# A gated cross-attention and expert kernel: layer 0's score operands in two row tiles, maxima and score halves placed side by side, gelu one sub-step later

## The chip, the core and the metric

The kernel runs on one core of a Trainium2 chip. The metric is device time in microseconds of that core; lower is better. TensorE (PE) multiplies and writes PSUM; VectorE (DVE), ScalarE (ACT) and GpSimd (POOL) do the rest; the sync engine (SP) holds a queue that issues every DMA transfer in program order.

## What is computed

Two layers, each of a cross-attention and an expert FFN, on x of 16 batches x 56 rows x 128 and a context of 16 x 1500 x 128. Sixteen heads of 8.

```python
x = x + tanh(g_xattn[0]) * xattn0(layernorm(x), ctx)            # no mask
x = x + tanh(g_ffn[0])   * ffn0(layernorm(x))                   # 8 experts of 512, top 2, exact gelu
x = x + tanh(g_xattn[1]) * xattn1(layernorm(x), ctx, mask)      # mask over the 1500 keys
x = x + tanh(g_ffn[1])   * ffn1(layernorm(x))                   # 8 experts of 64, and a shared one
# xattn: softmax(q k^T / sqrt(8)) v, heads joined, @ Wo + bo
```

## The kernel before

Batches go through in 32 steps: step n is batch n % 16 of layer n // 16, and steps run two at a time in a pipeline. In step s PE takes the maxima of batch s, the scores of batch s-1 (with a tail of batch s-2), weighs V with the exponentials, projects K for batch s+1 and V for batch s, and on odd and even steps does the small work of the FFN of the two batches that came before (`fy_uses`, `fh_uses`: experts `y0` to `y3`, hidden parts `h0` to `h7`, transposes, the query `q`).

A step has twelve sub-steps kt. Each has two maxima, two score halves and, in even kt, one weighing; K projections stand at kt 2, 4, 6 and V projections at kt 8, 9, 10.

- **Maximum** (`max_scores`, L1010): for one of 8 head pairs and one of 3 chunks of 500 keys, a matmul `qmax`^T `kop` into one of the two buffers of `pMX`. VectorE reduces it to a column of `mx` (L920, L925). 24 in a step. The maxima become shifts (`cc`, transposed to `ct`) that are written as two more rows of `qexp`.
- **Score half** (`score_half`, L972): the scores of 125 keys for four of the eight pairs, keys on the output's partitions, into one half of `pST`; ScalarE takes the exponential into `P` (L678). Half h of the next tile waits until half h is read.
- **Weighing** (`weigh`, L993): four matmuls of 17 columns at a time, on four column tiles, into `pO`.
- **Projection** (L1115 K, L1124 V) into the single `pKV`, which ScalarE copies out (L691, L696).

Queries and keys are split in a high and a low half float, so an operand has three blocks of 16 rows (a pair is 2 heads of 8): `kop` = khi, klo, khi and `qmax` = qhi, qhi, qlo. Behind them stand 56 mask rows and 2 shift rows, in layer 0 too, where the mask rows are zero: a maximum has 104 rows, a score 106. `kop`, `qmax` and `qexp` have two buffers, taken by n % 2.

SP's order in a step: the shifts to `qexp` (L474), the third part of the keys (L462), `qmax` copied to `qexp` (L486), the next context (L493), the first part of the next batch's keys, `qmax` of the next batch (L508, six transfers), the second part of the keys. The first part of the keys waits for the last score half of kt 6, which frees its buffer; the first maximum of the next step waits for `qmax` (`qmax_in`) and these keys (`kop_in[0]`).

In even steps from 4 on, kt 10 has the experts' second matmuls: `y0`, a maximum, `y1` (L1082), which wait for gelu. ScalarE does gelu at the end of kt 8, between two loads of its function table (L715, L678).

## Time and profile before

| | |
|---|---|
| median of 3 runs | 1040.72 us (1039.66 to 1044.62) |
| the profiled execution, its own time | 1040.23 us |
| its span, first to last instruction | 1038.1 us |
| TensorE busy / load of weights | 89% / 65% |
| VectorE, ScalarE, GpSimd busy | 70%, 56%, 51% |
| mean share of the 16 DMA engines | 49% |
| granted TensorE clock, mean | 0.981 |

The spans in this table and all views below are of one profiled execution. A row's duration for a matmul reaches to its modelled end, while the next one already runs; what a matmul costs PE is the distance from its start to the next start. "[1.17 <-ACT HR L715]" is idle time of the engine ahead of the row, and what ended it. SPq is the issue of a transfer on the SP queue, not the transfer. The granted clock is 1.00 from 200 us to the last matmuls.

### The profile page before, as it was taken

How to read it: one execution, taken by the hardware profiler on the slowest of the kernel's cores; microseconds unless marked ns; L12 is line 12 of the kernel's file. 1: busy time of each engine (PE TensorE's matmuls, PEld its weight loads, DVE VectorE, ACT ScalarE, POOL GpSimd, SP SyncE). 2: the span in 40 equal slices, each digit the busy share in tenths (PEclk: the TensorE clock that was granted, in tenths of full speed). 3: DMA queues.
4: the chain of work that ended last, by engine and by line, in shares of the span. 5: the costliest groups of instructions: out<-in, count | busy, mean ns of one | idle time of the engine just before them, and what ended most of it. 6: DMA issues, size and time to landing. Idle time of an engine off the chain costs nothing.

```text
span 1038.1 us, 32346 instructions
## 1 busy us (share of the span) xinstructions
PE 922.5 (89%) x13088; PEld 675.9 (65%) x13088; DVE 723.0 (70%) x1531; ACT 586.2 (56%) x1060; POOL 525.0 (51%) x667
## 2 busy tenths in 40 slices
PE   2487899999999999999999999999999999999974
PEld 0154577777777777777777777666666666666753
DVE  3376576785767768586785867878787878787722
ACT  1044556556565565656547565665757575757560
POOL 5353445543546335453446565665657576672202
PEclk9998899999999999999999999999999999999995
DMA  8735653333323333233465646767676767665200
GB/s 181 133 90 137 145 126 72 72 83 69 63 55 85 70 77 76 37 81 70 95 137 88 143 110 132 162 123 156 124 152 122 145 130 146 137 137 97 52 2 18
DMA packets 95215, 107.24 MB, mean 103 GB/s; under 512 B 22394, under 2 KB 86972, under 8 KB 95068
## 3 DMA queue, kind: packets, MB, share of 16 engines
q1 hardware_dynamic: 95068, 105.19, 49.0%
q8 instruction: 103, 1.69, 0.8%
q14 instruction: 44, 0.36, 0.1%
HBM read 35.89 MB, written 0.46 MB: 35 GB/s over the span
## 4 chain that ended last, share of the span: by engine, by line
PE 66%; DVE 16%; ACT 9%; issue 5%; SPq 2%; DMA 1%; POOL 0%; POOLq 0%; ACTq 0%; DVEq 0%
PE pO L993 13%; PE pMX L1010 12%; PE pST L972 12%; PE pKV L1124 6%; PE pFY L1082 6%; PE pKV L1115 5%; PE pFH L1150 5%; DVE mx L925 4%; DVE mx L920 4%; ACT P L678 3%; DVE rden L839 3%; PE pFY L1047 2%; ACT HR L715 1%; PE pFY L1086 1%; ACT V L696 1%
## 5 line engine op out<-in xcount | busy, mean ns | idle before, releaser
L678 ACT ACTIVATE P<-pST 125x448 f32<-125x448 f32 x768 | 396.1, 542 | 349.9 <-PE pST L972 344.3
L925 DVE TENSOR_REDUCE mx<-pMX 112x1 f32<-112x500 f32 x384 | 258.4, 673 | 172.3 <-PE pMX L1010 172.1
L1010 PE MATMUL pMX<-kop,qmax 104*112 104x500 f16 x768 | 293.1, 392 | 44.7 <-DMA qmax<-qlo 18.5
L972 PE MATMUL pST<-qexp,kop 106*128 106x112 f16 (+1 forms) x3072 | 280.2, 214 | 19.9 <-ACT P L678 9.3
L972 PEld LDWEIGHTS pST<-qexp,kop 106*128 106x128 f16 (+1 forms) x3072 | 209.9, 102 | 127.1 <-issue 42.9
L920 DVE TENSOR_REDUCE mx<-pMX 112x1 f32<-112x500 f32 x384 | 255.8, 666 | 42.8 <-PE pMX L1010 41.9
L993 PE MATMUL pO<-P,V 125*17 125x112 f32 x6144 | 186.0, 262 | 0.0
L993 PEld LDWEIGHTS pO<-P,V 125*17 125x17 f32 x6144 | 136.8, 98 | 46.2 <-issue 36.3
L1010 PEld LDWEIGHTS pMX<-kop,qmax 104*112 104x112 f16 x768 | 99.0, 132 | 93.1 <-issue 21.7
L563 POOL CAST khi<-kfull 128x500 f16<-128x500 f32 x96 | 57.7, 601 | 193.0 <-ACT kfull L691 192.8
L565 POOL TENSOR_TENSOR klo<-kfull,khi 128x500 f16<-128x500 f32 x96 | 109.0, 1135 | 7.8
L654 POOL TENSOR_TENSOR Clo<-C,Chi 128x500 f16<-128x500 f32 x93 | 105.8, 1138 | 7.5
L691 ACT ACTIVATE kfull<-pKV,W 128x500 f32<-128x500 f32 x96 | 65.0, 677 | 49.2 <-PE pKV L1115 41.1
L652 POOL CAST Chi<-C 128x500 f16<-128x500 f32 x93 | 56.6, 608 | 54.9 <-PE pKV L1124 43.8
L610 POOL TENSOR_TENSOR OM<-OM,rden 128x224 f32<-128x224 f32 x32 | 21.1, 658 | 119.6 <-DVE rden L839 119.6
L1150 PE MATMUL pFH<-xnfT,w1a 128*128 128x112 f32 x512 | 71.6, 283 | 0.0
L1124 PE MATMUL pKV<-Whi,Chi 128*128 128x128 f16 (+1 forms) x384 | 70.9, 222 | 0.7
L1082 PE MATMUL pFY<-w2a,HR 128*112 128x128 f32 x512 | 62.4, 275 | 9.4 <-ACT HR L715 9.4
L1124 PE MATMUL pKV<-Whi,Clo 128*128 128x128 f16 (+1 forms) x384 | 70.4, 221 | 0.0
L1124 PE MATMUL pKV<-Wlo,Chi 128*128 128x128 f16 (+1 forms) x384 | 70.3, 221 | 0.0
L1082 PEld LDWEIGHTS pFY<-w2a,HR 128*112 128x112 f32 x512 | 58.3, 177 | 11.5 <-issue 11.2
L696 ACT ACTIVATE V<-pKV 125x512 f32<-125x512 f32 x96 | 57.3, 597 | 14.5 <-PE pKV L1124 5.6
(144 smaller groups left out, 1089.6 us busy)
## 6 DMA issues: line engine op xcount, KB each, us to landing
C<-in_ctxT SPq DMA_DIRECT2D x32, 750.0 KB, 6.2
kop<-khi SPq DMA_DIRECT2D x192, 125.0 KB
kop<-maskop SPq DMA_DIRECT2D x48, 437.5 KB
kop<-klo SPq DMA_DIRECT2D x96, 125.0 KB
qexp<-qmax SPq DMA_DIRECT2D x32, 182.0 KB
maskin<-in_mask SPq DMA_DIRECT2D x8, 656.2 KB, 6.2
kop<-maskop SPq DMA_DIRECT2D x2, 1312.5 KB
qmax<-qhi SPq DMA_DIRECT2D x128, 7.0 KB
```

Of the source, the lines that this page charges most:

```text
L565: nc.gpsimd.tensor_tensor(klo[:, cols], kfull[:, c, :], khi[:, cols], ALU.subtract).then_inc(klo_done, 1)
L654: nc.gpsimd.tensor_tensor(Clo[:, s % 2, cols], C[:, cols], Chi[:, s % 2, cols], ALU.subtract).then_inc(ctx_split, 1)
L678: nc.scalar.activation(P[0:KP, slot, h * 4 * T:(h + 1) * 4 * T], pST[0:KP, h, 0:4 * T], ACT.Exp, scale=EXP_SCALE).then_inc(exp_done, 1)
L696: nc.scalar.activation(V[0:KP, s % 2, 4 * c:4 * c + 4, :, 0:PR].rearrange("k t p i -> k (t p) i"), pKV[0:KP, :].rearrange("k (m i) -> k m ...
L920: nc.vector.tensor_reduce(mx[:, s % 2, m // PAIRS, m % PAIRS:m % PAIRS + 1], pMX[0:T, 0, 0:CW], AX.X, ALU.max).then_inc(max_done, 1)
L925: nc.vector.tensor_reduce(mx[:, s % 2, m // PAIRS, m % PAIRS:m % PAIRS + 1], pMX[0:T, 1, 0:CW], AX.X, ALU.max).then_inc(max_done, 1)
L972: mm = nc.tensor.matmul(pST[0:cols, h, i * T:(i + 1) * T], kop[0:ROWS, b, p, tile * KP:tile * KP + cols], qexp[0:ROWS, b, p, :, :].rearran ...
L993: mm = nc.tensor.matmul(pO[32 * g:32 * g + VW, r * T:(r + 1) * T], V[0:KP, b, tile, p, :], P[0:KP, tile % RING, p * T:(p + 1) * T], start= ...
L1010: nc.tensor.matmul(pMX[0:T, m % 2, 0:CW], qmax[0:SHIFT0, st.s % 2, p, :, :].rearrange("r j q -> r (j q)"), kop[0:SHIFT0, st.s % 2, p, c * ...
L1082: mm = nc.tensor.matmul(o, HR[:, F0C * e + c, :], w2a[:, e, c, :], start=(c == 0), stop=(c == F0C - 1))
L1124: mm = nc.tensor.matmul(pKV[0:rows, i * D:(i + 1) * D], x_[:, s % 2, cols], m[:, l, 1, :], start=(k == 0), stop=(k == 2))
L1150: mm = nc.tensor.matmul(pFH[:, c * T:(c + 1) * T], w1a[:, e, c * 128:(c + 1) * 128], xnfT[:, :], start=True, stop=True)
```

## The change

In layer 0 the operands lose the mask rows and have 48 rows (50 with the shifts). Pairs 0 to 3 stand in rows 0 to 49, pairs 4 to 7 in rows 64 to 113, so `kop`, `qmax` and `qexp` use half their free size there, and a matmul touches one half of the rows. The weights' columns are put in that order at the start. Every transfer that fills these operands in layer 0 is now two, one for each half; layer 1's two shift rows and its query mask rows are written when batches 16 and 17 come. The fills of mask and pick at the start go.

On PE, a layer 0 sub-step is: a maximum of rows 64 on, the score half of rows 0 on, weighing, projection, a maximum of rows 0 on, the score half of rows 64 on, small work. Where the experts `y0`, `y1` stand (kt 10 of even steps, both layers), the projection comes before them and both score halves after them. ScalarE does gelu at the end of kt 9 instead of kt 8, and at kt 10 of even steps copies V before the exponential. `XF0` goes (its value is put in `xnf`).

```diff
+SHIFT0_L0 = 3 * PR
+ROWS_L0 = SHIFT0_L0 + 2
+HALF = 64
+HP = PAIRS // 2
+SHW = CW // 2
...
+def opens_layer(n):
+
+    return n in (B, B + 1)
+
+
+def b_total(n, c):
+
+    return sum(96 if layer_of(t) == 0 else 80 if opens_layer(t) and c == CH - 1 else 64 for t in range(n + 1))
+
+
+def q_total(n):
+
+    return sum(192 if layer_of(t) == 0 else 112 if opens_layer(t) else 96 for t in range(n + 1))
+
+
+def qexp_total(n):
+
+    return sum(32 if layer_of(t) == 0 else 16 for t in range(n % 2, n + 1, 2))
...
-            sp.wait_ge(init_v, 1)
-            sp.wait_ge(init_p, 5)
+            sp.wait_ge(init_p, 2)
             for b in range(2):
-                sp.dma_start(kop[MASK0:SHIFT0, b, :, :],
-                             maskop[0:S, :].unsqueeze(1).broadcast_to([S, PAIRS, S2])).then_inc(init_dma, 16)
-                for i in range(2):
-                    sp.dma_start(kop[SHIFT0 + i:SHIFT0 + i + 1, b, :, :],
-                                 shift_rows[:, i:i + 1, :].broadcast_to([1, PAIRS, S2])).then_inc(init_dma, 16)
-                sp.dma_start(qmax[MASK0:SHIFT0, b, :, :, :],
-                             pick[:, :, :].rearrange("s (p j) q -> s p j q", j=2)).then_inc(init_dma, 16)
+                for h in range(2):
+                    row = HALF * h + SHIFT0_L0
+                    sp.dma_start(kop[row:row + 2, b, 0:HP, :].rearrange("r p (i n) -> r (p i) n", n=SHW),
+                                 shift_rows[:, :].unsqueeze(1).broadcast_to([2, HP * S2 // SHW, SHW])
+                                 ).then_inc(init_dma, 16)
...
-                    sp.dma_start(kop[row:row + PR, dst, :, cols], part[:, cols]).then_inc(kop_in[c], 16)
+                    if n < B:
+                        for h in range(2):
+                            at = HALF * h + row
+                            sp.dma_start(kop[at:at + PR, dst, 0:HP, cols], part[HALF * h:HALF * (h + 1), cols]
+                                         ).then_inc(kop_in[c], 16)
+                    else:
+                        sp.dma_start(kop[row:row + PR, dst, :, cols], part[:, cols]).then_inc(kop_in[c], 16)
                 if n >= B:
                     half = S * (n % 2)
                     sp.dma_start(kop[MASK0:SHIFT0, dst, :, cols],
                                  maskop[half:half + S, cols].unsqueeze(1).broadcast_to([S, PAIRS, CW])
                                  ).then_inc(kop_in[c], 16)
+                if opens_layer(n) and c == CH - 1:
...
-                    sp.dma_start(qexp[SHIFT0:ROWS, (s - 1) % 2, :, :, :].rearrange("r p j q -> r (p j q)"),
-                                 ct[:, :]).then_inc(shift_in, 16)
+                    for h in range(2):
+                        if layer_of(s - 1) == 0:
+                            row = HALF * h + SHIFT0_L0
+                            to = qexp[row:row + 2, (s - 1) % 2, 0:HP, :, :]
+                        else:
+                            to = qexp[SHIFT0:ROWS, (s - 1) % 2, HP * h:HP * (h + 1), :, :]
+                        sp.dma_start(to.rearrange("r p j q -> r (p j q)"), ct[PAIRS * h:PAIRS * (h + 1), :]
+                                     ).then_inc(shift_in, 16)
...
-                    sp.dma_start(qexp[0:SHIFT0, s % 2, :, :, :], qmax[0:SHIFT0, s % 2, :, :, :]).then_inc(qexp_in[s % 2], 16)
+                    if layer_of(s) == 0:
+                        for h in range(2):
+                            rows = slice(HALF * h, HALF * h + SHIFT0_L0)
+                            sp.dma_start(qexp[rows, s % 2, 0:HP, :, :], qmax[rows, s % 2, 0:HP, :, :]
+                                         ).then_inc(qexp_in[s % 2], 16)
+                    else:
+                        sp.dma_start(qexp[0:SHIFT0, s % 2, :, :, :], qmax[0:SHIFT0, s % 2, :, :, :]
+                                     ).then_inc(qexp_in[s % 2], 16)
...
-                            sp.dma_start(qmax[row + HD * j:row + HD * (j + 1), (s + 1) % 2, :, j, :],
-                                         part[64 * j:64 * (j + 1), half:half + S]).then_inc(qmax_in, 16)
+                            if s + 1 < B:
+                                for h in range(2):
+                                    at, of = HALF * h + row + HD * j, HALF * h + HALF // 2 * j
+                                    sp.dma_start(qmax[at:at + HD, (s + 1) % 2, 0:HP, j, :],
+                                                 part[of:of + HALF // 2, half:half + S]).then_inc(qmax_in, 16)
+                            else:
+                                sp.dma_start(qmax[row + HD * j:row + HD * (j + 1), (s + 1) % 2, :, j, :],
+                                             part[64 * j:64 * (j + 1), half:half + S]).then_inc(qmax_in, 16)
+                    if opens_layer(s + 1):
+                        sp.dma_start(qmax[MASK0:SHIFT0, (s + 1) % 2, :, :, :].rearrange("s p j q -> s (p j) q"),
+                                     pick[:, :].unsqueeze(1).broadcast_to([S, H, S])).then_inc(qmax_in, 16)
...
+                for kt in range(KT):
+                    side_by_side = False
+                    if has_f(s) and kt == 10:
+                        evacuate(kt)
+                    exps(st, kt, 0)
+                    if not side_by_side and not (has_f(s) and kt == 10):
+                        evacuate(kt)
                     exps(st, kt, 1)
+                    if side_by_side and not (has_f(s) and kt == 10):
+                        evacuate(kt)
...
-                    if kt == 8 and has_f(s):
+                    if kt == 9 and has_f(s):
...
+                def largest(m):
+
+                    c, i = divmod(m, PAIRS)
+                    p = HP * (1 - m % 2) + i // 2 if layer_of(s) == 0 else i
+                    nc.vector.tensor_reduce(mx[:, s % 2, c, p:p + 1], pMX[0:T, m % 2, 0:CW], AX.X, ALU.max
+                                            ).then_inc(max_done, 1)
...
+                for i in range(HP):
+                    if layer_of(n) == 0:
+                        rows, slot = slice(HALF * h, HALF * h + ROWS_L0), i
+                    else:
+                        rows, slot = slice(0, ROWS), HP * h + i
+                    mm = nc.tensor.matmul(pST[0:keys.stop - keys.start, h, i * T:(i + 1) * T],
+                                          kop[rows, b, slot, keys],
+                                          qexp[rows, b, slot, :, :].rearrange("r j q -> r (j q)"),
...
+                if layer_of(n) == 0:
+                    h = 1 - m % 2
+                    rows, slot = slice(HALF * h, HALF * h + SHIFT0_L0), i // 2
+                else:
+                    rows, slot = slice(0, SHIFT0), i
+                nc.tensor.matmul(pMX[0:T, m % 2, 0:CW], qmax[rows, b, slot, :, :].rearrange("r j q -> r (j q)"),
+                                 kop[rows, b, slot, c * CW:(c + 1) * CW], start=True, stop=True).then_inc(mx_ready, 1)
...
+                    m0 = MAXES_PER_KT * kt
+                    together = has_m(s) and layer_of(s) == 0
+                    apart_ = has_m(s) and layer_of(s) == 1
                     late = kt in (1, 7)
-                    if has_m(s) and not late:
-                        max_scores(st, MAXES_PER_KT * kt)
-                    weigh(st, kt)
                     experts = [u[1] for u in fy_uses(s) if u[0] == kt and early(u[1])]
                     if experts:
+                        if has_m(s):
+                            max_scores(st, m0)
+                        weigh(st, kt)
+                        project(kt)
                         small("y0")
                         if has_m(s):
-                            max_scores(st, MAXES_PER_KT * kt + 1)
+                            max_scores(st, m0 + 1)
                         small("y1")
-                    score_half(st, kt, 0)
-                    if has_m(s) and late:
-                        max_scores(st, MAXES_PER_KT * kt)
-                    for use in [u[1] for u in kv_uses(s) if u[0] == kt]:
-                        c = int(use[1])
-                        free(kv_free, kv_uses, use)
-                        if use[0] == "k":
-                            if s == -1:
-                                pe.wait_ge(init_c, 2 * LAYERS + c + 1)
-                            else:
-                                pe.wait_ge(ctx_split, st.at(lambda s: CH * s + c + 1))
-                            b, l, cols = (s + 1) % 2, layer_of(s + 1), slice(c * CW, (c + 1) * CW)
-                            for i, (m, x_) in enumerate(((Whi, Chi), (Whi, Clo), (Wlo, Chi))):
-                                mm = nc.tensor.matmul(pKV[:, 0:CW], m[:, l, 0, :], x_[:, b, cols],
-                                                      start=(i == 0), stop=(i == 2))
-                        else:
-                            l = layer_of(s)
-                            for i in range(KPC):
-                                first = (KPC * c + i) * KP
-                                rows = min(KW, S2 - first)
-                                cols = slice(first, first + rows)
-                                for k, (x_, m) in enumerate(((Chi, Whi), (Chi, Wlo), (Clo, Whi))):
-                                    mm = nc.tensor.matmul(pKV[0:rows, i * D:(i + 1) * D], x_[:, s % 2, cols], m[:, l, 1, :],
-                                                          start=(k == 0), stop=(k == 2))
-                        mm.then_inc(kv_ready, 1)
-                    if has_m(s) and not experts:
-                        max_scores(st, MAXES_PER_KT * kt + 1)
-                    score_half(st, kt, 1)
+                        score_half(st, kt, 0)
+                        score_half(st, kt, 1)
+                    elif together:
+                        max_scores(st, m0)
+                        score_half(st, kt, 0)
+                        weigh(st, kt)
+                        project(kt)
+                        max_scores(st, m0 + 1)
+                        score_half(st, kt, 1)
```

The first place is kt 6 of an even step of layer 0 on PE (pMX is a maximum, pST a score half, pO a weighing, pKV a projection). Before:

```order
L1010 MATMUL pMX<-kop,qmax 112x500
L993 MATMUL pO<-P,V 17x112 x16
L972 MATMUL pST<-qexp,kop 128x112 x4
L1115 MATMUL pKV<-Chi,Whi 128x500
L1115 MATMUL pKV<-Clo,Whi 128x500
L1115 MATMUL pKV<-Chi,Wlo 128x500
L1010 MATMUL pMX<-kop,qmax 112x500
```

And after the change:

```order
L1109 MATMUL pMX<-kop,qmax 112x500
L1067 MATMUL pST<-qexp,kop 128x112 x4
L1088 MATMUL pO<-P,V 17x112 x16
L1141 MATMUL pKV<-Chi,Whi 128x500
L1141 MATMUL pKV<-Clo,Whi 128x500
L1141 MATMUL pKV<-Chi,Wlo 128x500
L1109 MATMUL pMX<-kop,qmax 112x500
L1067 MATMUL pST<-qexp,kop 128x112 x4
```

The score half has moved ahead of the weighing, next to the first maximum. The second place is kt 10 of an even step on PE; pFY are `y0` and `y1`. Before:

```order
L1010 MATMUL pMX<-kop,qmax 112x500
L993 MATMUL pO<-P,V 17x112 x16
L1082 MATMUL pFY<-w2a,HR 112x128 x8
L1010 MATMUL pMX<-kop,qmax 112x500
L1082 MATMUL pFY<-w2a,HR 112x128 x8
L972 MATMUL pST<-qexp,kop 128x112 x4
```

And after the change, from the last matmuls of the projection on:

```order
L1150 MATMUL pKV<-Wlo,Chi 125x128
L1150 MATMUL pKV<-Whi,Clo 125x128
L1204 MATMUL pFY<-w2a,HR 112x128 x8
L1109 MATMUL pMX<-kop,qmax 112x500
L1204 MATMUL pFY<-w2a,HR 112x128 x8
L1067 MATMUL pST<-qexp,kop 128x112 x8
```

The projection stood between the two score halves and stands now ahead of `y0`; the halves come together at the end. The third place is the SP queue of one step of layer 0, from the next context to the second part of the keys. Before:

```order
L493 DMA C<-in_ctxT 128x1500
L462 DMA kop<-khi 16x8x500
L462 DMA kop<-klo 16x8x500
L462 DMA kop<-khi 16x8x500
L508 DMA qmax<-qhi 8x8x56 x4
L508 DMA qmax<-qlo 8x8x56 x2
L462 DMA kop<-khi 16x8x500
```

And after the change:

```order
L540 DMA C<-in_ctxT 128x1500
L489 DMA kop<-khi 16x4x500 x2
L489 DMA kop<-klo 16x4x500 x2
L489 DMA kop<-khi 16x4x500 x2
L560 DMA qmax<-qhi 8x4x56 x8
L560 DMA qmax<-qlo 8x4x56 x4
L489 DMA kop<-khi 16x4x500 x2
```

Each transfer has become two of half the pairs.

## Rows read from the trace of the kernel before

**Rows 1.** The page, busy time of each engine (us, share, instructions).
```profile
PE 922.5 (89%) x13088; PEld 675.9 (65%) x13088; DVE 723.0 (70%) x1531; ACT 586.2 (56%) x1060; POOL 525.0 (51%) x667
```
**Rows 2.** Windows: an odd and an even step of layer 0, first maximum to first maximum.
```profile
305.20:335.50 30.30, 29.48 (x432) 22.78 (x430) 22.24 (x48) 16.62 (x33) 16.04 (x24) 1.00 0.38 83
335.50:368.50 33.00, 30.84 (x443) 24.33 (x441) 23.57 (x49) 20.59 (x33) 13.21 (x17) 1.00 0.29 58
```
**Rows 3.** The chain that ended last, from 76.1 us (start, us, what).
```profile
76.13 0.20 PE pST L972 x4
76.33 0.21 PE pMX L1010
...
76.74 0.71 PE pKV L1124 x12
```
**Rows 4.** Timeline, TensorE, a sub-step with weighing (start, us, engine, line, what).
```profile
352.04 0.38 PE L1010 MATMUL pMX<-kop,qmax 104*112 104x500 f16 x1
352.34 0.96 PE L993 MATMUL pO<-P,V 125*17 125x112 f32 x32
353.24 0.37 PE L972 MATMUL pST<-qexp,kop 106*128 106x112 f16 x4
```
**Rows 5.** Timeline, TensorE, two matmuls of 9 rows and what follows.
```profile
318.61 0.47 PE L1066 MATMUL pFY<-b2x,gateT 9*112 9x128 f32 x2
319.00 0.32 PE L1138 MATMUL pFH<-ident,xnq 112*128 112x112 f32 x1
```
**Rows 6.** Timeline, VectorE, two maxima with work waiting.
```profile
354.50 0.67 DVE L925 TENSOR_REDUCE mx<-pMX 112x1 f32<-112x500 f32 x1
355.10 0.68 DVE L920 TENSOR_REDUCE mx<-pMX 112x1 f32<-112x500 f32 x1
```
**Rows 7.** Timeline, SP queue, end of step 11; TensorE, first maximum of step 12.
```profile
386.89 0.56 SPq L462 DMA_DIRECT2D kop<-khi  x1
...
391.68 1.26 SPq L508 DMA_DIRECT2D qmax<-qlo  x2
...
398.78 0.38 PE L1010 MATMUL pMX<-kop,qmax 104*112 104x500 f16 x1
```
**Rows 8.** Lines 508 and 462, issue time in ns (min/median/max).
```profile
L508 SPq DMA_DIRECT2D qmax<-qhi x128: 608/620/1912, 29.6 to 950.8; - x128
...
L462 SPq DMA_DIRECT2D kop<-khi x192: 547/593/1361, 27.5 to 963.7; - x192
```
**Rows 9.** DMA issues with us to landing; the chain's piece for the first qmax.
```profile
out<-X SPq DMA_DIRECT2D x1, 56.0 KB, 1.6
...
32.92 5.14 DMA qmax<-qlo
```
**Rows 10.** Timeline, TensorE, the first maximum and the idle time before it.
```profile
38.11 1.08 PE L1010 MATMUL pMX<-kop,qmax 104*112 104x500 f16 x2 [18.54 <-DMA qmax<-qlo]
```
**Rows 11.** Timeline, SP queue, end of step 2; TensorE, first maximum of step 3.
```profile
109.17 1.26 SPq L508 DMA_DIRECT2D qmax<-qlo  x2
...
112.57 0.39 PE L1010 MATMUL pMX<-kop,qmax 104*112 104x500 f16 x1
```
**Rows 12.** Timeline, TensorE and ScalarE, sub-steps 9 and 10 of step 10.
```profile
358.22 0.60 ACT L696 ACTIVATE V<-pKV 125x512 f32<-125x512 f32 x1
358.43 0.38 PE L1010 MATMUL pMX<-kop,qmax 104*112 104x500 f16 x1
358.72 0.54 ACT L678 ACTIVATE P<-pST 125x448 f32<-125x448 f32 x1
359.27 1.28 ACT L715 ACT_TABLE_LOAD   x1
360.57 3.28 ACT L715 ACTIVATE HR<-HR 128x1792 f32<-128x1792 f32 x2
362.41 1.97 PE L1082 MATMUL pFY<-w2a,HR 128*112 128x128 f32 x16 [1.17 <-ACT HR L715]
367.25 0.38 PE L1010 MATMUL pMX<-kop,qmax 104*112 104x500 f16 x1
```

204 lines of the change are left out of this document (126 added, 78 removed).

## The prediction

> **What bounds the kernel now.** I read the page first: TensorE (PE) is busy for 89% of the span [rows 1], so PE should bound. Matmuls overlap in that figure, so I went on to the windows of two steps of layer 0, one odd and one even [rows 2]: PE 29.5 of 30.3 us and 30.8 of 33.0, VectorE (DVE) 22.2 and 23.6. Then the timeline of PE, by the distance from one start to the next. There the chain that ended last gives the price of each piece: a maximum 0.21 us, a score half of four matmuls 0.20, a V projection of twelve 0.71 [rows 3]. DVE takes 0.60 us from one maximum to the next when it has work waiting [rows 6], and pMX has two buffers. A sub-step with two maxima thus cannot run faster than about 1.2 us for long, whatever PE does, while two maxima and two score halves cost PE only 0.82. Last, the SP queue: in layer 0 it issues the keys' first part and then six qmax transfers, the last of which starts at 391.68 + 0.63 = 392.31; the next step's first maximum, which needs them, starts at 398.78, 6.5 us later [rows 7]. That slack is what the change spends.
>
> **Part 1, side by side.** Layer 0 puts a maximum (rows 64 to 113, or 0 to 49) directly before the score half on the other 50 rows. The trace of before has no two row tiles at once. Its nearest row is the weighing: 32 matmuls of 17 columns, four to a group on four column tiles, take 0.90 us from 352.34 to 353.24 [rows 4]; one by one at about 0.1 each they would take 3.2. So tiles of the array do run together here. Bounds for a pair of maximum and score half: 0.21 us (fully together) and 0.42 (one after the other). In between, if the five weight loads go one by one at the 0.05 us at which score matmuls follow each other, 0.26. I take 0.21: column tiles are the only packing the trace shows and it is nearly whole. Gain 0.21 a pair, 24 pairs in an odd step: 5.0 us.
>
> **Part 2, more changes of shape.** The array's tiling now changes between row halves (maximum, score), column tiles (weighing) and the whole array (projection, FFN). Its price stands in rows: from the maximum to the weighing there are 0.30 us instead of 0.21 [rows 3, 4]. Two matmuls of 9 rows (a row tile of their own) take 0.39 up to the next start, where two f32 ones of 128 columns take 0.23 (16 in about 1.81 us, the 1.97 of the row less one's tail) [rows 5, 12]: 0.16 with the weight load laid bare. I take 0.10, bounds 0 and 0.16; 0.10 since maxima and score halves are half floats like those of rows 4. By the order of after I count 23 more changes in an odd step and 22 in an even one (a projection after a weighing adds one, each whole-array matmul group between two score halves adds two): 2.3 and 2.2 us.
> The Trainium skill, "TensorEngine Tiling (Array Packing)", Key Properties, says that changing the tiling mode, not just the tile, drains TensorE, and that tiles then load and multiply in parallel. The drain agrees with the 0.10 us of rows 4; the parallel run of row tiles is shown by no row. Were a change free, an odd step's sum would be 5.0 us down; with the drain it is 2.7.
>
> **Part 3, DVE and ACT stay.** In bare sub-steps (kt 7 and 11 of an even step) the gain is nothing, since DVE's 2 x 0.60 us already fill them. Around kt 5 to 7 DVE also has the reciprocal and the copies; I charge 0.5 us a step for maxima that now wait (bounds 0 and 1.5). An odd step on PE and DVE: -5.0 + 2.3 + 0.5 = -2.2 us.
>
> **Part 4, gelu one sub-step later** (even steps). Now sub-step 9 starts at 358.43, ScalarE's table load at 359.27, gelu at 360.57, and y0 at 362.41 after a wait of 1.17; sub-step 11 starts at 367.25 [rows 12]. On ScalarE a copy of V takes 0.50 to the next start and an exponential 0.55 [rows 12]. After: maximum with score 0.21, change 0.1, projection 0.7 and 0.15 until its last result, copy of V 0.5, exponential 0.55: 2.2 us after the sub-step's start; table load 1.3, half of gelu 1.64: y0 at +5.4 instead of +3.98. PE is there at about +3.2, so it waits 2.2 us instead of 1.17, although the second projection now lies in that time. From y0 on: 1.81 + 0.1 + 0.21 + 0.1 + 1.75 + 0.1 + 0.42 = 4.5, so sub-step 11 starts at +9.9 instead of +8.82: +1.1 us. Two score halves then stand back to back, so kt 11 waits for exponentials and gains nothing. Even step: pairs in kt 0 to 6 and 8, 8 x 0.42 = -3.4; 15 changes there, +1.5; kt 9 and 10 +1.1; DVE +0.5: -0.3 us.
> In layer 1 there are no row tiles, and the later gelu alone costs: about 1 us in steps 16 and 18, which still have layer 0's FFN, and 0.15 in each of six further even steps: +3.
>
> **Part 5, the SP queue.** Each transfer of layer 0 becomes two of half the size: 18 kop transfers a step instead of 9, 12 qmax instead of 6, 2 + 2 instead of 1 + 1. An issue takes 0.59 us for kop (128 pieces of 1000 bytes) and 0.61 to 0.62 for qmax (64 pieces of 112) [rows 8]: half the pieces and a small part of the bytes save nothing, so I let halved ones cost the same. From the keys' release to the last qmax issue: now 386.89 to 392.31, 5.4 us; after, 3 more kop at 0.62 and 6 more qmax at 0.65 (median and the gap to the next): 5.4 + 1.9 + 3.9 = 11.2. Landing takes between 1.6 us (56 KB, alone) and 5.1 (the last qmax of the crowded start) [rows 9]; I take 2.0, near the former, since the queue in mid-run is nearly empty. The operands are there 13.2 us after the release. PE gets to the next step's first maximum 398.78 - 386.89 = 11.9 us after it now; with five sub-steps' gain (-2.1) and 13 changes (+1.3) at 11.1. **The wait is 2.1 us and takes the odd step's gain whole.** Behind it on PE stand all of the step's matmuls; behind the issues on SP stand the second key part and the shifts, wanted 8 us later. At the end of an even step the experts lie in that stretch (358.43 to 367.25 alone is 8.8 us [rows 12], with sub-steps 7, 8 and 11 besides), so nothing waits. A pair of steps comes out at -2.2 + 2.1 - 0.3 = -0.4 us; six pairs (steps 4 to 15): -2.
>
> **Part 6, the opening.** The first maximum waits 18.5 us for qmax, which stood behind the mask and pick fills, and starts at 38.11 [rows 10]. Those fills go, but 12 qmax issues come. Keys and queries should be there near 19 us (an estimate: PE's last matmuls before that wait end at 38.11 - 18.5 = 19.6): six kop and 12 qmax issues and the landing give 19 + 3.7 + 0.2 + 7.8 + 2.0 = 32.7, some 5 us earlier. The queue is then late for the shifts of step 0 (8 small loads stand in it), which leaves about 2. Before step 3 the slack is least: last issue at 109.17 + 0.63 = 109.80, maximum at 112.57, so 0.8 us after landing [rows 11], and the queue now needs 5.9 more; before step 2 I take one of 1.7, twice that (an estimate from those rows, step 1 being as bare). Lateness of some 4 and 5 us, less what the earlier sub-steps gain (1.5 each) and the 2 of the start, and 1 at step 4: +5 (bounds -2 and +9).
>
> **Sum.** +5 (opening), -2 (six pairs), +3 (later steps): +6 us on the profiled span of 1038.1, 1044.1. That execution took 1040.2 as a whole and the median of the runs is 0.5 higher, so 1046.7: **1047 us**, 0.6% slower. 0.5% (5 us) is about what a measurement of this kernel can tell from no change.
>
> **Rivals.**
> (a) The halved issues are cheap, half of 0.6 us: the queue is in time everywhere, and the odd steps keep their 2.2. Then opening -6, first steps -1, six pairs of -2.2 - 0.3, later steps +3: -19, **1022 us**. It decides from about 0.5 us an issue downward (18 issues have to save 2.1 us). For it speaks that no row has a halved transfer; against it, that the issue time of rows 8 is the same for 128 pieces as for 64. This is the case on the other side. Chance 0.2.
> (b) Row tiles don't run together; a pair stays 0.42. Then odd steps +2.3 and the queue is just in time, even ones +3.4 (more in kt 9 to 11), 34 in six pairs, opening +9, later +3: **1087 us**. For it: no row shows two row tiles at once; against it: the column tiles of rows 4. Chance 0.1.
> (c) Weight loads one by one, 0.26 a pair: +1.2 a step, half of it hidden under the queue's wait: +10, **1057 us**. Chance 0.15.
> (d) The queue is late as said, but DVE's waits fall into it and into PE's others (-1.0 a pair, -6), and the opening comes out even (-5): **1036 us**. Chance 0.2.
> My own case (1040 to 1053): 0.35.
> The Trainium skill, "TensorE: Matmul & The Clock Gate", Measured speedup vs the span model, gives a pack the time of its longest matmul plus some 4 ns a tile: by that a pair is 0.22 us and (b) does not happen; no row has two row tiles, so nothing above leans on it.
>
> **Numbers.** Left out of the range: (b) and the cheap end of (a), some 2 in 10: 1024 to 1066; the likeliest case's own is 1040 to 1053. Faster by over 0.5% (under 1035.5): (a) and nearly half of (d), 0.29; slower (over 1046): (b), (c) and over half of mine, 0.47; within: 0.24.
>
> **What would show it.** Right if, in layer 0, a score half's first matmul starts within 0.02 us of the maximum ahead of it and the next maximum 0.21 after; if some 0.1 us stands at each change of shape; if the first maximum of even steps waits about 2 us for qmax while that of odd ones doesn't; if y0 waits 2.2 us for gelu; if SP's issues stay at 0.6 us. The issue time is the weakest step: it turns the sign. Next is the opening, where late small transfers of step 0 and 1 can cost or free 5 us.

## The result and the profile after

The changed kernel took 1116.9 us (median of 4 runs, 1115.5 to 1121.9) beside 1042.1 us for the kernel before on the same chip (4 runs): a ratio of 1.073, 95% interval 1.068 to 1.077. It is 7% slower. The forecast was 1047 us, slower by 0.6%: the sign was right, the size was wrong by far. One execution of experiment 1 and one of experiment 8 ran over 1.5% above the fastest of their kernel; they are left out of the medians and ratios below.

The page after has TensorE's busy time and, as tenths in 40 slices, the clock that it was granted; it answers to [rows 1]:

```profile
PE 952.9 (85%) x13088; PEld 676.8 (61%) x13088; DVE 725.5 (65%) x1537; ACT 586.3 (53%) x1060; POOL 519.7 (47%) x666
...
PEclk9995888989989799899999999999999999999975
```

The same number of matmuls, yet TensorE is busy for 30 us more: some of them ran slower, though pairs overlap now. The mean granted clock is 0.933 (before 0.981). The windows show where (columns as in [rows 2]: length, busy time of PE, its weight loads, DVE, ACT, POOL, granted clock, DMA share, GB/s). The first row is steps 0 to 4, the second is step 7, the third is the start of step 8:

```profile
30.30:208.00 177.70, 136.94 (x1507) 85.57 (x1508) 96.87 (x197) 68.71 (x124) 66.03 (x78) 0.83 0.31 91
276.50:309.00 32.50, 27.98 (x433) 20.67 (x429) 23.96 (x53) 16.53 (x33) 17.60 (x25) 1.00 0.20 65
309.00:322.00 13.00, 12.98 (x132) 9.57 (x132) 5.74 (x11) 3.90 (x8) 1.15 (x2) 0.61 0.11 35
```

For 13 us at the start of step 8 the granted clock is 0.61. The timeline of TensorE there shows what it did before:

```profile
304.58 0.41 PE L1109 MATMUL pMX<-kop,qmax 48*112 48x500 f16 x1
304.58 0.37 PE L1067 MATMUL pST<-qexp,kop 50*128 50x112 f16 x4
304.79 0.37 PE L1109 MATMUL pMX<-kop,qmax 48*112 48x500 f16 x1
...
305.36 1.15 PE L1271 MATMUL pFH<-xnfT,w1a 128*128 128x112 f32 x8 [0.17 <-DVE HR L879]
308.99 0.41 PE L1109 MATMUL pMX<-kop,qmax 48*112 48x500 f16 x1 [2.49 <-DMA qmax<-qlo]
...
309.34 1.16 PE L1088 MATMUL pO<-P,V 125*17 125x112 f32 x32
310.42 0.66 PE L1109 MATMUL pMX<-kop,qmax 48*112 48x500 f16 x1
...
311.20 2.05 PE L1271 MATMUL pFH<-xnfT,w1a 128*128 128x112 f32 x8
```

Three things are to be seen. A score half starts with its maximum, and the next maximum 0.21 us after the first (304.58 to 304.79): the pairs do run side by side. Then TensorE idles 2.49 us for qmax. And 1.4 us behind that wait the clock is at its lower level: a maximum takes 0.66 instead of 0.41 to its end, eight f32 matmuls of a hidden part 2.05 instead of 1.15 (1.2 instead of 2.4 GHz). It is back at 320.3, where the same eight take 1.15 again.

The SP queue ahead of that wait, beside [rows 7] (before, the last issue started 5.4 us behind the keys' release):

```profile
294.56 1.23 SPq L489 DMA_DIRECT2D kop<-khi  x2
...
298.60 6.39 SPq L560 DMA_DIRECT2D qmax<-qhi  x8
305.04 2.81 SPq L560 DMA_DIRECT2D qmax<-qlo  x4
```

The last issue starts at 307.18, 12.6 us behind the keys' release at 294.56, and ends at 307.85; the operands are there at 308.99.

The starts of the steps (their first maximum) show how the 77.6 us of the two profiled spans add up. In layer 0 beyond the opening (steps 5 to 14) an odd step takes 32.35 us (30.23 before) and an even one 37.3 (33.06 before). Step 15, behind which no wait for qmax stands, takes 30.15.

| start of | before | after | difference |
|---|---|---|---|
| step 0 | 38.1 | 30.3 | -7.8 |
| step 5 | 178.7 | 208.0 | +29.3 |
| step 16 | 525.4 | 586.5 | +61.1 |
| step 18 | 588.8 | 654.0 | +65.2 |
| step 31 | 956.3 | 1027.8 | +71.5 |
| end | 1038.1 | 1115.7 | +77.6 |

### The profile page after: what moved, and what is told of

The parts are those of the page before. It is cut to its first block, busy times and chain, and to the rows that moved or that the text cites. A ratio compares the mean times of both kernels' runs of the same rounds, so it can differ in the third digit from the quotient of the medians.

```text
span 1115.7 us, 32642 instructions
## 1 busy us (share of the span) xinstructions
PE 952.9 (85%) x13088; PEld 676.8 (61%) x13088; DVE 725.5 (65%) x1537; ACT 586.3 (53%) x1060; POOL 519.7 (47%) x666
## 4 chain that ended last, share of the span: by engine, by line
PE 57%; DVE 17%; SPq 10%; issue 7%; ACT 6%; DMA 2%; POOL 1%; POOLq 0%; DVEq 0%
PE pO L1088 12%; PE pMX L1109 9%; PE pST L1067 9%; DVE mx L973 9%; PE pFY L1204 6%; SPq L560 6%; PE pKV L1141 5%; PE pFH L1271 5%; PE pKV L1150 4%; SPq L489 4%; DVE rden L915 2%; PE pFY L1208 2%; ACT P L736 2%; ACT HR L784 1%; PE pFY L1163 1%
## 5 line engine op out<-in xcount | busy, mean ns | idle before, releaser
L973 DVE TENSOR_REDUCE mx<-pMX 112x1 f32<-112x500 f32 x768 | 494.2, 669 | 271.8 <-PE pMX L1109 269.2
L1109 PE MATMUL pMX<-kop,qmax 48*112 48x500 f16 (+1 forms) x768 | 300.8, 424 | 67.0 <-DVE mx L973 29.0
L1067 PE MATMUL pST<-qexp,kop 50*128 50x112 f16 (+2 forms) x3072 | 281.3, 221 | 25.2 <-issue 14.6
L1067 PEld LDWEIGHTS pST<-qexp,kop 50*128 50x128 f16 (+2 forms) x3072 | 191.8, 103 | 93.0 <-issue 40.0
L1088 PE MATMUL pO<-P,V 125*17 125x112 f32 x6144 | 200.1, 275 | 0.0
L1109 PEld LDWEIGHTS pMX<-kop,qmax 48*112 48x112 f16 (+1 forms) x768 | 98.9, 132 | 160.1 <-issue 54.5
L1088 PEld LDWEIGHTS pO<-P,V 125*17 125x17 f32 x6144 | 146.0, 102 | 38.1 <-issue 20.6
L1271 PE MATMUL pFH<-xnfT,w1a 128*128 128x112 f32 x512 | 82.7, 311 | 2.6 <-DVE HR L879 2.6
L750 ACT ACTIVATE kfull<-pKV,bkp 128x500 f32<-128x500 f32 x48 | 32.5, 677 | 91.0 <-PE pKV L1141 91.0
L1271 PEld LDWEIGHTS pFH<-xnfT,w1a 128*128 128x128 f32 x512 | 72.1, 216 | 8.3 <-DVE HR L879 5.7
L1150 PE MATMUL pKV<-Whi,Clo 128*128 128x128 f16 (+1 forms) x384 | 71.5, 223 | 0.0
L1150 PE MATMUL pKV<-Wlo,Chi 128*128 128x128 f16 (+1 forms) x384 | 71.5, 223 | 0.0
```

Of the source, the lines that this page charges most:

```text
L973: nc.vector.tensor_reduce(mx[:, s % 2, c, p:p + 1], pMX[0:T, m % 2, 0:CW], AX.X, ALU.max).then_inc(max_done, 1)
L1067: mm = nc.tensor.matmul(pST[0:keys.stop - keys.start, h, i * T:(i + 1) * T], kop[rows, b, slot, keys], qexp[rows, b, slot, :, :].rearrange ...
L1088: mm = nc.tensor.matmul(pO[32 * g:32 * g + VW, r * T:(r + 1) * T], V[0:KP, b, tile, p, :], P[0:KP, tile % RING, p * T:(p + 1) * T], start= ...
L1109: nc.tensor.matmul(pMX[0:T, m % 2, 0:CW], qmax[rows, b, slot, :, :].rearrange("r j q -> r (j q)"), kop[rows, b, slot, c * CW:(c + 1) * CW] ...
L1150: mm = nc.tensor.matmul(pKV[0:rows, i * D:(i + 1) * D], x_[:, s % 2, cols], m[:, l, 1, :], start=(k == 0), stop=(k == 2))
L1271: mm = nc.tensor.matmul(pFH[:, c * T:(c + 1) * T], w1a[:, e, c * 128:(c + 1) * 128], xnfT[:, :], start=True, stop=True)
```

## The experiments

Times are medians; each ratio is to the kernel before on the same chip, with its 95% interval. Step lengths are differences of first maxima in one profiled execution.

**1. Maximum and score half on the same rows.** The maxima of a sub-step swap their halves, so that each lies on the rows of the score half behind it.

```diff
-                    h = 1 - m % 2
+                    h = m % 2
```

> In layer 0 the maximum directly ahead of a score half now lies on the same 50 rows as that half (the order of the two halves among the maxima is swapped), so two row tiles are never at work at once; layout, transfers and order stay those of the changed kernel. If row tiles run side by side as the trace shows (pair 0.21 us), a pair now costs 0.42: +5.0 us an odd step, of which the 2.4 us of waiting for qmax takes half, and +3.4 us an even one: about +36 us over six pairs of steps and some +5 in the opening, 1117 + 40 = 1155 us. Rival: VectorE's 0.60 us a maximum already sets the pace of most sub-steps, so the side by side order gives little: +10 us or less, 1127. Rival: the pairs only look parallel in the records: no change, 1117.

1143.7 us, ratio 1.098 (1.090 to 1.105): 27 us more than the changed kernel, where 38 were expected. The timeline of TensorE at the end of step 7 and the start of step 8:

```profile
312.68 0.42 PE L1109 MATMUL pMX<-kop,qmax 48*112 48x500 f16 x1
312.93 0.21 PE L1067 MATMUL pST<-qexp,kop 50*128 50x112 f16 x1
312.94 0.41 PE L1109 MATMUL pMX<-kop,qmax 48*112 48x500 f16 x1
...
315.44 0.41 PE L1109 MATMUL pMX<-kop,qmax 48*112 48x500 f16 x1 [0.81 <-DMA qmax<-qlo]
315.69 0.36 PE L1067 MATMUL pST<-qexp,kop 50*128 50x112 f16 x4
315.98 0.96 PE L1088 MATMUL pO<-P,V 125*17 125x112 f32 x32
```

The score half now starts 0.25 us behind its maximum, and the pair takes 0.54 us up to the weighing (315.44 to 315.98), 0.35 in the changed kernel (308.99 to 309.34). The pairs are parallel work, not an artefact of the records. But the edit does not part row tiles everywhere, as it was meant to: where two pairs stand in a row, the half of the first and the maximum of the second now lie on different rows and start together (312.93 and 312.94). Step 15, which has no wait for qmax behind it and the full clock in both kernels, takes 32.24 us instead of 30.15. Its matmuls take 3.4 us more (31.4 instead of 28.0), less than the 5.0 of 24 pairs, since some still overlap; of these, 1.3 come back, because TensorE's waits, VectorE's maxima above all, fall from 2.1 to 0.8. An even step at the full clock differs by 1.6 us (sub-steps 0 to 9 of step 8: 25.5, and 23.8 in experiment 3), where 3.4 were expected. The odd steps 5 to 13 take 34.8 us instead of 32.35: their wait for qmax falls from 2.4 to 1.2, but in steps 5, 7, 9 and 11 sub-step 6 runs at 1.2 GHz and takes 5.0 us instead of the 3.5 of steps 13 and 15. Behind the wait of 0.81 the weighing (315.98 to 316.88) runs at the full clock and sub-steps 0 and 1 take 5.1 us instead of 7.1. The rival that the pairs only look parallel falls. The one that VectorE hides the saving falls by size, but in step 15 some 40% of what the pairs save does come back as waits.

**2. Half of the qmax transfers from ScalarE's queue.**

```diff
+                    if kt in (7, 8, 9) and s + 1 < B:
+                        query_part((7, 8, 9).index(kt))
```

> Six of the twelve qmax transfers of a layer 0 step (those of rows 64 on) are issued from ScalarE's queue, two behind the exponentials of sub-steps 7, 8 and 9 each, instead of from SP. SP's chain from the keys' release to the last qmax issue is 3.9 us shorter. Theory (late queue, and the granted clock falls to 1.2 GHz after the wait): the 2.4 us wait ahead of the first maximum of even steps goes, and with it the stretch at 0.61 behind it, about 4 us: 6 x 6.4 = 38 us, and some 8 in the opening: 1117 - 46 = 1071 us; granted clock 1.00 in the first 13 us of even steps. Rival 1 (the clock falls by itself, for instance because half-filled row tiles keep the array less busy): only the waits go, 14 + 5 us: 1098, clock still 0.61 there. Rival 2 (the landing, not the issue, is late): no change, 1117.

1087.8 us, ratio 1.045 (1.041 to 1.050): 29 us less than the change. Odd steps take 30.45 us, the wait for qmax is gone from step 5 on and sub-steps 0 to 2 of even steps run at 1.00. Rivals 1 and 2 fall. But even steps still take 36.5 us, and the timeline of TensorE in sub-step 10 of step 8 says why:

```profile
315.90 2.43 PE L1222 MATMUL pFY<-w2a,HR 128*112 128x128 f32 x16 [2.82 <-ACT HR L802]
318.26 0.66 PE L1127 MATMUL pMX<-kop,qmax 48*112 48x500 f16 x1
318.86 2.87 PE L1222 MATMUL pFY<-w2a,HR 128*112 128x128 f32 x16
```

ScalarE's own issues push gelu back, y0 waits 2.82 us (1.97 in the changed kernel), and in steps 6, 8 and 12 the clock falls behind this wait: y1 takes 2.87 instead of 2.00. In steps 10 and 14 it does not, behind waits of 2.82 and 3.22. Against an even step without either (33.7, experiment 3) that is some 3 us in the mean, which the expected 1071 did not have.

**3. Matmuls in the wait.** The wait stays, its idleness goes.

```diff
+                if m == 0 and n % 2 == 0 and 4 <= n < B:
+                    pe.wait_ge(max_done, NMAX * n - 1)
+                    for _ in range(8):
+                        nc.tensor.matmul(pMX[0:T, 0, 0:CW], Whi[:, 0, 0, 0:T],
+                                         Whi[:, :, :, :].rearrange("p l m n -> p (l m n)")[:, 0:CW],
+                                         start=True, stop=True)
```

> The changed kernel with eight extra matmuls of 500 columns on constant operands (1.7 us at 2.4 GHz, result never read) ahead of the first maximum of steps 4, 6, ... 14, where TensorE waits 2.4 us for qmax. The operands land when they did, so nothing is gained from the wait itself. Theory (the idle wait lets the granted clock fall): the stretch behind it stays at 2.4 GHz and about 4 us a step come back: 1117 - 24 = 1093 us, with the wait shown as 0.5 to 0.8 instead of 2.4. Rival 1 (the clock falls for another reason): 1117, still 0.61 in the 13 us behind. Rival 2 (extra matmuls only add): up to +2.

1102.0 us, ratio 1.057 (1.054 to 1.060): 15 us less, by adding work. TensorE at the start of step 8, and the window behind it:

```profile
303.17 1.85 PE L1101 MATMUL pMX<-Whi 128*112 128x500 f16 x8
305.25 0.41 PE L1115 MATMUL pMX<-kop,qmax 48*112 48x500 f16 x1 [0.23 <-DMA qmax<-qlo]
...
305.59 0.96 PE L1088 MATMUL pO<-P,V 125*17 125x112 f32 x32
...
306.97 1.15 PE L1277 MATMUL pFH<-xnfT,w1a 128*128 128x112 f32 x8
```
```profile
305.20:318.00 12.80, 12.34 (x188) 9.28 (x189) 8.77 (x19) 5.89 (x12) 2.06 (x3) 1.00 0.20 64
```

The window's clock is 1.00 where the changed kernel has 0.61, and it holds 188 matmul records instead of 132. The operands and the row tiles are the same, so it is the idle wait that lets the clock fall here. Even steps take 33.7 us instead of 37.3 wherever nothing else happens: the clock alone costs 3.6 us a step. In steps 6, 10 and 14 it fell behind the 1.97 us wait for gelu instead, which costs 1.6 (35.3), and step 4 gained nothing (43.3 us, 43.2 in the changed kernel); that is why 24 us were expected and 15 came.

**4. Gelu back at sub-step 8**, with the old order of sub-step 10.

```diff
-                    if kt == 9 and has_f(s):
+                    if kt == 8 and has_f(s):
```

> The changed kernel with gelu back at the end of sub-step 8 and sub-step 10 of even steps back in the order of before (projection and copy of V between the two score halves), in both layers; row tiles, transfers and the order of all else stay. Theory (Part 4: y0 waits about 1 us longer and the half scores come late): 1.2 us in each of six even steps of layer 0 and 0.8 in each of eight in layer 1: 1117 - 14 = 1103 us. Rival: what y0 gains is given back because the queue's late qmax, 2.4 us in the next odd to even change, is fixed to another event, and in layer 1 VectorE fills it: 1115 to 1117.

1092.1 us, ratio 1.048 (1.043 to 1.053): 25 us less, where 14 were expected. From step 18 to the end the span takes 450.1 us (changed kernel 461.7, before 449.3): the late gelu costs 11.6 us there, some 5 of them in the last step and behind it, where y0 waits 1.72 us instead of 0.72 and the clock is low afterwards. The rest is in layer 0, 12.4 us of it in steps 5 to 15, and part of that is the clock and not gelu: in steps 8 and 12 it stayed at 2.4 GHz behind waits for qmax of 1.92 and 1.96 us.

**5. Both repairs**, four of the twelve transfers on ScalarE's queue and in odd steps only (and before step 4).

> Both repairs on the changed kernel: gelu back at sub-step 8 with the old order of sub-step 10, and four of the twelve qmax transfers issued from ScalarE's queue (two each in sub-steps 7 and 8), but in odd steps and before step 4 only, so that nothing stands ahead of gelu. Theory (the losses are the late queue, the clock behind waits, and gelu; the row tiles themselves give almost nothing, since a maximum costs VectorE 0.60 us and sub-steps without a projection stay at 1.5 to 1.7): odd steps of layer 0 come to 30.0 us, even ones to 33.1, as long as before (30.3 and 33.0); only the opening is some 9 us shorter: 1033 us. Rival (the saving of Part 1 and 2 of the prediction is there once the queue is in time, 2.2 us an odd step and 1.9 an even one): 1010 us. Rival (another wait takes the queue's place): over 1050.

1068.8 us, ratio 1.027 (1.021 to 1.032). Odd steps take 30.13 us as expected, even ones 34.0 (33.1 expected); of the 36 us above the expected 1033, most are in the opening (step 5 starts at 190.9). Beyond the opening nothing waits long and the clock is 1.00, and still a pair of steps takes 64.2 us, 63.3 before. The side by side work pays nothing here. One part is this experiment's own: ScalarE's issues lengthen sub-step 10 of odd steps to 4.15 us (3.63 before). TensorE's timeline in sub-step 4 of step 9 shows another reason:

```profile
330.03 0.39 PE L1126 MATMUL pMX<-kop,qmax 48*112 48x500 f16 x1 [0.92 <-DVE mx L990]
...
330.34 0.96 PE L1105 MATMUL pO<-P,V 125*17 125x112 f32 x32
331.24 0.39 PE L1158 MATMUL pKV<-Chi,Whi 128*128 128x500 f16 x1
...
331.97 0.41 PE L1126 MATMUL pMX<-kop,qmax 48*112 48x500 f16 x1
...
332.32 0.47 PE L1205 MATMUL pFY<-b2x,gateT 9*112 9x128 f32 x2
```

The K projection takes 0.73 us to the next maximum (331.24 to 331.97), 0.63 before; the pair behind it takes 0.35 to the next whole-array matmul (331.97 to 332.32), where two pairs in a row are 0.21 apart. So a change costs 0.10 us into the pairs and 0.14 out of them. Summed by kind over one odd step (step 9 of both kernels, start to next start less the waits): maxima and score halves took 11.3 us before and 8.3 now (2.9 less), all projections and small matmuls 12.8 before and 14.3 now (1.4 more), and the waits 0.8 before and 2.2 now (1.4 more). The weighing stays at 5.4.

**6. The issues alone**, in the kernel before: its layout and order, each layer 0 transfer of kop and qmax cut in two by rows.

```diff
+                            for h in range(2):
+                                at = row + HD * j + 4 * h
+                                sp.dma_start(qmax[at:at + 4, (s + 1) % 2, :, j, :],
+                                             part[64 * j + 32 * h:64 * j + 32 * (h + 1), half:half + S]
```

> The kernel before with its own layout and order, and only the issues of the change: in layer 0 each kop and qmax transfer becomes two of half the rows (8 and 8, 4 and 4), so 18 kop and 12 qmax issues a step. Theory (late queue): the last qmax lands 13.2 us behind the keys' release, TensorE is there at 11.9: a wait of 1.3 us before each even step, too short for the clock to fall (a wait of 1.97 for gelu left it at 1.00, one of 2.8 did not), so 6 x 1.3 = 8 us, and 5 to 10 in the opening: 1058 us. Rival 1 (the clock falls behind this wait too): 6 x 4 more, 1082. Rival 2 (issues cost nothing by themselves, it is the row tile layout that makes the transfers slow): 1042 to 1045.

1081.9 us, ratio 1.039 (1.034 to 1.043). Timeline of SP and TensorE at the end of step 9:

```profile
357.91 1.30 SPq L469 DMA_DIRECT2D kop<-khi  x2
...
362.09 5.39 SPq L521 DMA_DIRECT2D qmax<-qhi  x8
367.52 2.63 SPq L521 DMA_DIRECT2D qmax<-qlo  x4
...
371.34 0.42 PE L1027 MATMUL pMX<-kop,qmax 104*112 104x500 f16 x1 [1.38 <-DMA qmax<-qlo]
```

13.4 us from release to first maximum and a wait of 1.38 us, as worked out (13.2 and 1.3), with no fall of the clock behind it: 1.6 us a pair of steps, the 8 expected. (Step 12 had a wait of 1.71, a fall of the clock and 1.9 us more.) But the total is 40 us, not 16. The rest is in the opening: step 5 starts at 209.8 instead of 178.7. So the doubled issues alone, without row tiles, cost 31 us before step 5.

**7 and 8. VectorE's pace taken away.** Each maximum is taken over 250 of its 500 keys (half of every reduction is left out), in the kernel before and in that of experiment 5.

```diff
-                    nc.vector.tensor_reduce(mx[:, s % 2, c, p:p + 1], pMX[0:T, m % 2, 0:CW], AX.X, ALU.max
+                    nc.vector.tensor_reduce(mx[:, s % 2, c, p:p + 1], pMX[0:T, m % 2, 0:CW // 2], AX.X, ALU.max
```

> The kernel before, with VectorE taking each maximum over the first 250 of the 500 keys only (half of each reduction's work is left out, in both layers); TensorE's work is all there. It is the control of the next run: what VectorE's pace alone costs without row tiles. A reduction should take about 0.34 us to the next start instead of 0.60. If VectorE paces the sub-steps without projections (1.5 to 1.7 us where TensorE needs 0.82 and small work), some 6 of them in a step lose 0.3 to 0.5: 2 to 3 us a step, 1042 - 32 x 2.5 = 962 us. If TensorE bounds as its 89% say: 1035 to 1042.

> The kernel of e5 with the same half reductions as e7 (half of each maximum's keys left out on VectorE). Compared with e7 it tells what row tiles give where VectorE doesn't pace. Theory: the saving of some 2 to 4 us a step in layer 0 that VectorE hides in e5 comes out: 16 x 3 = 48 us less than e7 in layer 0, while e5 is only some 9 us (the opening) below before. Rival (the change of tiling or the exponentials, not VectorE, eat the saving): e8 is below e7 by no more than e5 is below before, some 10 us.

The kernel before comes to 1017.9 us (ratio 0.977, 0.973 to 0.982), that of experiment 5 to 1043.0 (1.001, 0.998 to 1.005): 24 and 26 us less. Of the first 80 were expected, so VectorE sets the pace of the kernel before far less than I had it; and the kernel with row tiles was to be 48 us below it, and is 25 above. In layer 0 a pair of steps (7 to 11) takes 29.9 + 32.7 = 62.6 without row tiles and 29.6 + 33.0 = 62.6 with them. My theory that VectorE hides the saving falls: with half its work gone the 0.9 us by which row tiles were behind are gone, but row tiles still give nothing. This kernel carries the 0.5 us of ScalarE's issues in an odd step too, which is far less than what is missing. The rest goes into changes of tiling and into waits for other things.

**9 and 10. The late loads one step later**, behind the next context, on top of experiment 5 and alone on the kernel before. Experiment 9 also moves ScalarE's second pair of qmax transfers ahead of the copy of V in sub-step 8, so its difference to experiment 5 is that of two edits.

```diff
                     sp.dma_start(C[:, :], ctxT[(s + 2) % B]).then_inc(c_in, 16)
+                late_loads(s - 1)
...
-                late_loads(s)
```

> The kernel of e5 with two further moves in SP's and ScalarE's order. The late loads (output weights, experts' weights, mask) are issued one step later, behind the next context, so that the shifts of the next step no longer stand behind them on SP; and the second pair of ScalarE's qmax transfers goes ahead of the second copy of V in sub-step 8 instead of behind its exponentials. Theory (of e5's 27 us over before, nearly all are in the opening: steps 2 to 4 take 35.2, 33.7, 42.7 with 4 to 9 us in sub-step 3, where the scores wait for shifts, at a granted clock of 0.80): step 5 starts 15 to 20 us earlier than at 190.9, and sub-step 10 of odd steps is 3.63 again instead of 4.15: 1069 - 21 = 1048 us. Rival (the loads themselves, not their place, are late): 1065 or more.

> The control of e9: the kernel before with only the late loads issued one step later, behind the next context. Its sub-step 3 of steps 2 and 3 takes 5.6 and 5.0 where later ones take 1.6 to 1.9. Theory: some 6 us are to be had there without any row tile: 1042 - 6 = 1036 us. Rival (it waits for the transfers of keys and context, not for shifts): 1042.

1054.6 us (ratio 1.011, 1.005 to 1.016) and 1033.0 (0.989, 0.984 to 0.993). Sub-step 3 of steps 2 and 3 shrinks to 1.3 and 1.6 us with row tiles (6.5 and 4.1 in experiment 5) and to 1.6 and 1.4 without (5.6 and 5.0). Sub-step 10 of odd steps is 3.63 again (4.15 in experiment 5). 1048 and 1036 were expected. So 10 us are to be had in the kernel before with no row tile at all. In steps 5, 7 and 13 of experiment 9 the clock falls, and sub-step 1 takes 4.6 to 5.0 us instead of 3.0. Where it does not, steps 8 and 9 take 62.9 us and steps 10 and 11 63.3, beside 63.3 before: without the misplaced issues row tiles come out about even.

**11. Both pairs of a sub-step together**, on top of 9. ScalarE copies the projection behind both exponentials.

```diff
                         max_scores(st, m0)
                         score_half(st, kt, 0)
-                        weigh(st, kt)
-                        project(kt)
                         max_scores(st, m0 + 1)
                         score_half(st, kt, 1)
+                        weigh(st, kt)
+                        project(kt)
```

> The kernel of e9 with both pairs of a sub-step put together in layer 0 (maximum, half 0, maximum, half 1, then weighing, projection and small work; ScalarE copies the projection behind both exponentials), sub-step 10 of even steps as it was. Theory (the saving of the pairs goes into changes of tiling, measured at 0.13 us out of a pair and 0.11 into one, 28 to 30 of them in an odd step): a sub-step has two changes fewer wherever something lies between its pairs, some ten times in a step, 2.4 us a step: 16 x 2 = 32 us less than e9. Rival (VectorE gets its two maxima at once and ScalarE its two halves, and then both idle; what the changes save comes back as waits): within 5 us of e9.

1025.0 us, ratio 0.983 (0.979 to 0.986): 30 us less than experiment 9 (32 expected) and faster than the kernel before. Odd steps take 28.9 us (30.23 before), even ones 32.7 (33.06). TensorE's timeline, sub-step 6 of step 9:

```profile
304.50 0.41 PE L1132 MATMUL pMX<-kop,qmax 48*112 48x500 f16 x1
...
305.03 0.41 PE L1132 MATMUL pMX<-kop,qmax 48*112 48x500 f16 x1
305.03 0.37 PE L1090 MATMUL pST<-qexp,kop 50*128 50x112 f16 x4
305.37 0.96 PE L1111 MATMUL pO<-P,V 125*17 125x112 f32 x32
306.27 0.38 PE L1164 MATMUL pKV<-Chi,Whi 128*128 128x500 f16 x1
...
306.91 0.37 PE L1286 MATMUL pFH<-xnqT,W 128*128 128x112 f32 x2
```

The projection is followed by other whole-array work and takes 0.64 again. That 30 met the 32 is mostly luck, for these were to be 2 us in every step of layer 0. Of the 30 us, 16 lie ahead of step 5, where experiment 9 waits longer and at a lower clock; I have not taken them apart. Beyond it this kernel has none of the three falls of the clock of experiment 9, and where that one has none either, the order saves some 1.5 us a pair of steps (28.9 instead of 29.7 to 30.0, and 32.7 instead of 33.1 to 33.8). Experiment 10, on the same chip, stands at 1033.0 and its interval touches this one's (0.984 to 0.993), so the advantage over it is best read in the steps: 1.7 us in each of five pairs of layer 0, of which steps 16 and 17 give back 3 (66.5 us instead of 63.4), since there full-height maxima stand beside row tile scores.

**12. The late loads alone** on the changed kernel.

> The changed kernel with only the late loads issued one step later, behind the next context; everything else, the twelve qmax issues on SP and the late gelu too, stays. It tells how much of the opening's loss (step 5 starts at 208.0 instead of 178.7) is the shifts' place behind the late loads and how much is the qmax queue. Theory (both: sub-step 3 of steps 2 to 4 takes 6.6, 4.0 and 6.3 us for shifts, sub-step 11 of steps 2 and 3 and the waits for qmax stay, with the low clock behind them): steps 2 to 4 lose 4.7 + 2.4 + 4.4 = 11.5 us of stall and a few us of low clock: 1117 - 14 = 1103 us, with six waits of 2 to 2.5 us for qmax and the low clock behind them as they were. Rival (the shifts are late because the qmax issues make the whole queue late): 1112 to 1117.

1104.3 us, ratio 1.058 (1.050 to 1.065): 13 us less, as expected. Step 5 starts at 193.5 instead of 208.0, 14.5 us earlier. But the same move makes step 5 start 7.9 us earlier in the kernel before too (experiment 10: 170.8 instead of 178.7). So 6.6 of the 29.3 us that the change loses in the opening are the place of the loads; the other 22.7 are there with the loads moved in both.

## Why the prediction was wrong, step by step

**Where the 72 us are.** The forecast had +6 on the profiled span, and it is +77.6: +29.3 where +5 stood for the opening, +31.8 where -2 stood for the further steps of layer 0, and +16.5 where +3 stood for what comes behind.

**A pair costs 0.21 us (Part 1): right, but its ground and its worth were not.** Both the timeline (304.58 to 304.79) and experiment 1 show the 0.21. No row shows the 0.1 us for one matmul of 17 columns by which the weighing was taken as proof that tiles run together; [rows 4] have 0.90 us for 32, and nothing there tells packed from one by one. And not all of what pairs save shortens a step: experiment 1 adds 3.4 us of matmul time to step 15 and only 2.1 to its length, the rest being waited for in the changed kernel.

**0.10 us a change of tiling (Part 2): nearly right, somewhat low.** 0.10 into the pairs and 0.14 out, as the sub-step of experiment 5 shows. It is the sum of Parts 1 to 3 that fails: on TensorE and VectorE an odd step was to gain 2.2 us, and it gains 0.25 (32.35 less the mean wait of 2.4, against 30.23). By the sums of experiment 5, maxima and halves save 2.9 us where Part 1 had 5.0, so that 2.1 go into the changes out of a pair; the matmuls behind them cost 1.4 more, mostly for the changes into one. That is 3.5 for both, and I had 2.3. The waits grow by 1.4, such as the 0.92 us in the rows of experiment 5, where Part 3 had 0.5. Experiments 7 and 8 show that halving VectorE's time for a maximum takes only a part of these waits away (they stay at 1.5 in step 9 of experiment 8, and at 0.6 in experiment 7); which other order of waits does the rest was not settled.

**Gelu later, +1.1 an even step (Part 4): right in layer 0, too small behind it.** Sub-steps 9 and 10 take 10.0 us (8.8 before), and y0 waits 1.97, where I had 2.2. (The terms written for y0 add up to +5.1 and not +5.4, and the row has +5.6, with TensorE there at +3.6 instead of +3.2: small errors that nearly cancel.) In layer 1 I put 0.15 on an even step; experiment 4 makes it 0.9 a pair of steps, and 5 us in the tail, where I had nothing. Steps 16 and 17 take 67.5 us together instead of 63.4, where I had 1; experiments 5 and 11 keep 3 of these 4, so that is the row tile scores beside full-height maxima rather than gelu. TensorE's row of y0 in step 8 of the changed kernel, beside [rows 12]:

```profile
341.14 1.97 PE L1204 MATMUL pFY<-w2a,HR 128*112 128x128 f32 x16 [1.97 <-ACT HR L784]
```

**The SP queue, a wait of 2.1 us (Part 5): right.** 1.95 to 3.04 us ahead of the even steps 6 to 14, mean 2.4. That it came so near is in part luck. In step 8 the last issue starts 12.6 us behind the release instead of 11.2 (the eight qhi issues alone take 6.39), and the operands are there 1.8 us later, near the 2.0 taken: 14.4 us instead of 13.2. But TensorE, too, comes later, 11.9 us behind the release instead of 11.1 and as late as in the kernel before, since the odd step gained nothing.

**The step that failed: what a wait costs.** I priced each wait at its own length. At these waits the granted clock drops from 2.4 to 1.2 GHz and stays there for 3 to 14 us (9 in the mean of steps 6 to 14), and this costs 3.6 us a step, more than the wait itself. Experiment 3 shows it by taking away the idleness alone. No part and no rival had it, although the trace of before held the sign: from 90 to 98 us, with waits of 2.1 and 4.1 us, its granted clock is 0.57. It is 18 of the 34 us that steps 5 to 15 were off. The pair of steps, in the prediction's terms:

| us in a pair of steps | predicted | measured |
|---|---|---|
| odd step on PE and DVE | -2.2 | -0.25 |
| wait for qmax | +2.1 | +2.4 |
| low clock behind it | not in the sum | +3.6 |
| even step but for gelu | -1.4 | -0.55 |
| gelu | +1.1 | +1.2 |
| sum | -0.4 | +6.4 |

The Trainium skill, "TensorE: Matmul & The Clock Gate", What's actually happening, has the low clock as the default and activity as what releases it; I had drawn on that page for the time of a pack alone. The rows of step 8 agree with it: 1.00 ahead of the idle 2.49 us, 0.61 behind. Which wait is followed by a fall is not told by its length alone (see the last section).

**The opening, +5 (Part 6): wrong by 24 us.** The first maximum is at 30.3, where I had 32.7. But step 5 starts 29.3 us late, and steps 0 to 4 take 37 us longer (177.7 against 140.6 us from the first maximum on). The waits of TensorE in them (us in total, times, longest):

```profile
PE pMX L1109 <- DMA qmax<-qlo: 15.8, 2, 11.5
PE pST L1067 <- issue: 12.6, 3, 5.8
PE pMX L1109 <- DVE mx L973: 8.8, 17, 0.8
PE pMX L1109 <- issue: 7.5, 2, 5.5
PE pST L1067 <- DMA qexp<-ct: 2.7, 1, 2.7
```

Without the 11.5 ahead of the first maximum all waits there come to 39.3 us, against 18.8 before: 20 us. TensorE's busy time, 136.9 against 121.1 us for as many matmuls (clock 0.83 against 0.95), is the other 16. I had looked at one transfer per step, the last qmax, and at its slack. The queue is what carries lateness on: in step 2 the shifts stand behind the late qmax issues, the second key part and six late loads, and the scores stop for them in sub-step 3. The timelines of SP and of TensorE there:

```profile
92.61 0.60 SPq L461 DMA_DIRECT2D w1a<-in_w  x1
93.25 0.64 SPq L462 DMA_DIRECT2D maskin<-in_mask  x1
94.02 1.44 SPq L514 DMA_DIRECT2D qexp<-ct  x2
...
95.84 0.41 PE L1109 MATMUL pMX<-kop,qmax 48*112 48x500 f16 x1 [0.49 <-DVE mx L973]
102.08 0.61 PE L1067 MATMUL pST<-qexp,kop 50*128 50x112 f16 x8 [5.83 <-issue]
```

Two shifts of 1.8 KB are issued at 94.0 behind 1024 KB of weights and 656 KB of mask, and the scores start at 102.1. Experiment 6 makes 31 us out of the doubled issues alone, as much as the whole loss. Experiment 12 gives 14.5 us back by moving those loads, of which 7.9 are to be had in the kernel before as well. That both act through late shifts and a low clock is read from these rows; how the rest divides among single waits was not tried.

**Behind step 15, +3: wrong by 13 us.** By experiment 4 the late gelu costs 11.6 us from step 18 on, and the row tile scores of steps 16 and 17 some 3.

**The rivals.** None of them was the case: issues stayed at 0.6 us against (a), pairs are parallel against (b) and (c), and (d) had the queue's lateness right and its price wrong.

## What to carry to other kernels

Price a new wait on TensorE by what follows it as well: here 2.4 us of idleness cost 6 in the mean, though not every such wait did. When one queue gets more issues, follow its order through to the next step's small transfers and not only to the one that is wanted first. Side by side row tiles pay when several such groups stand together; put between other work, they lost all of it again here in changes of tiling and waits.

## What the hardware showed that was not expected

- **The clock falls at one short wait, but not at each.** In steps 6 to 14 of the changed kernel it fell to 1.2 GHz at all five waits for qmax (1.95, 1.96, 2.42, 2.49 and 3.04 us), within the wait or up to 1.7 us behind it, and at none of the five waits of 1.97 for gelu. In the same steps of the other runs it fell at waits for qmax of 1.71 (experiment 6) and 1.40 (experiment 1), and not at 1.36 to 1.38 (experiment 6), 0.79 to 0.82 (experiment 1) or 1.92 and 1.96 (steps 8 and 12 of experiment 4, where it did at 1.96, 1.93 and 2.08 in steps 6, 10 and 14). It fell at the 1.97 for gelu in steps 6, 10 and 14 of experiment 3 and not in 8 and 12; at 2.82 in step 8 of experiment 2 and not in step 10. In experiment 9 it fell within 2 us behind waits of 1.18, 0.99 and 0.63.
- **It also fell with no wait close by.** In sub-step 6 of steps 5, 7, 9 and 11 of experiment 1 the granted clock is 0.50 (225.9 to 229.3 us in step 5), though TensorE's last wait of over 0.3 us, one of 0.66, ended 5 us earlier. Its cause stays open.
- **Extra matmuls in a wait make a kernel faster**: eight of them, six times, 15 us.
- **Two row tiles work at once with separate operands**: maximum and score half of four matmuls in 0.21 us where another pair follows. Where the weighing follows, the pair takes 0.35 us, and 0.54 on the same rows (experiment 1).
- **Halving a transfer halves nothing of its issue**: qmax 0.67 us for 32 pieces, 0.62 for 64 before; kop 0.59 both ways.
